# Turning raw images by products with diagonals of 1 / norm in the setup of a deformable-convolution kernel

## The chip, the core and the metric

The kernel runs on one core of one Trainium2 chip. Its time is the device time of one execution in microseconds (us). Engines are named as in the profile: PE (matmul; PEld its weight loads), DVE (vector), ACT (scalar), POOL (GpSimd) and SP (which only issues transfers here).

## The reference, cut to what matters

The input is 32 images of 64 channels and 16x16 pixels, float32. A first stage finds for every channel the partner that is least like it and normalises both together; two deformable convolution layers with batch norm follow.

```python
nrm = jnp.linalg.norm(x_flat, axis=2, keepdims=True)          # per image and channel, over 256 pixels
x_n = x_flat / jnp.maximum(nrm, 1e-12)
cos = jnp.einsum('bcn,bdn->cd', x_n, x_n) / B                  # 64x64, over all images and pixels
_, idx = jax.lax.top_k(-jnp.abs(cos).T, k)                     # k = 2, the second is the partner
gs = s + s[:, idx[:, 1:]].sum(axis=-1)                         # sums of channel and partner
gsq = sq + sq[:, idx[:, 1:]].sum(axis=-1)
...
x_hat = (x - mean) * inv                                       # then gamma, beta
# then twice: offsets by 3x3 convolution, deformable 3x3 convolution, batch norm, relu; residual at the end
```

## The kernel before, in words

Images go in pairs: the 128 partitions hold the 64 channels of one image above those of another, so there are 16 pairs ("t") of 128x256 values, read in four chunks of four pairs (`X_CHUNKS`). Everything up to the first pad of an image (L425) is called the setup here; it ends at about 26.5 us. The two layers behind it work pair by pair, their order is written out by hand, and the change doesn't touch them.

The setup has no scheduler: each engine runs its own list in the order of the code, and semaphores tie them.

- SP issues the four chunks of x, after the first one the identity matrix (64 KB), and after chunk 2 has landed the other constants.
- DVE takes statistics of each pair (`bn_stats`, L781), forms the sum of squares per chunk in three dependent steps (L788 to L793), and between the statistics of the next chunk finishes 1 / norm (L765, L768) and scales two of the four pairs (L773).
- ACT takes the root (`norm`, L404), scales the other two pairs (L410) and copies turned slabs out of PSUM (`copy_turned`, L399).
- PE, for each j of 8 (two pairs), turns the scaled slab with four 128x128 transposes (`turn`, L543) and, one j later, adds its gram products to PSUM (`gram`, L553): the order is turn(0), turn(1), gram(0), turn(2), gram(1), and so on to gram(7).
- Then a chain of small steps: the gram is copied, folded over the two images (L564), made minus its absolute value, its top 8 and their indices found (L801 to L809), the index made float (L811), compared with 0 to 63 in each half (L816), transposed on PE (L567), the identity added (L819), and the product with the sums made (L570).
- `keep_busy` makes PE multiply constants where it would otherwise wait.

One product in float32 stands in the profile as two matmul records, called passes here; a transpose stands as one.

Of the kernel before, what the change touches and what calls it, by code (L numbers as in the profile page):

```python
# [25 lines left out]
ALU = mybir.AluOpType  # L26
# [52 lines left out]
CONST_SIZES = dict(ident=P, fold=P, combine=2 * SLICE_PLACES, combine_taps=SLICE_PLACES, grid=PLACES, iota=C, edges=2)  # L79
# [26 lines left out]
def program(nc, x, consts, consts16, conv_w, conv_b, dcn_w, vecs, out):  # L106
# [3 lines left out]
    with ExitStack() as ctx:  # L110
# [38 lines left out]
        gram_sb = sb("gram_sb", [P, C])  # L149
# [3 lines left out]
        partner = sb("partner", [P, 1])  # L153
        pick = sb("pick", [P, P])
# [31 lines left out]
        iota = cst[:, CONSTS["iota"][0]:CONSTS["iota"][1]]  # L186
# [5 lines left out]
        xn = raw  # L192
        xn_t = S[:, 0, 0, :, :]

        x_in = [sem(f"x_in{i}") for i in range(X_CHUNKS)]
        ident_in = sem("ident_in")
# [9 lines left out]
        xn_by_act = sem("xn_by_act")  # L206
        xn_by_dve = sem("xn_by_dve")
# [65 lines left out]
        def _(sp):  # L273
            for g in range(X_CHUNKS):
                chunk = slice(g * CHUNK_PAIRS, (g + 1) * CHUNK_PAIRS)
                sp.dma_start(xs[:, chunk, :], x_dram[:, chunk, :]).then_inc(x_in[g], 16)
                if g == 0:
                    sp.dma_start(ident, consts[:, 0:CONSTS["fold"][0]]).then_inc(ident_in, 16)
            sp.wait_ge(x_in[X_CHUNKS - 2], 16)
            sp.dma_start(cst[:, CONSTS["fold"][0]:CONST_COLS], consts[:, CONSTS["fold"][0]:CONST_COLS]).then_inc(consts_in, 16)  # L280
# [18 lines left out]
            sp.wait_ge(cleared, 8)  # L299
# [20 lines left out]
        def _(pool):  # L320
            pool.memset(bc[:, :], 0.0).then_inc(cleared, 1)
            pool.memset(bc_centre[:, :], 0.0).then_inc(cleared, 1)
            pool.memset(pick[:, :], 0.0).then_inc(cleared, 1)
# [69 lines left out]
        def _(act):  # L393

            def copy_turned(j):
                act.wait_ge(xn_turned, j + 1)
                if j >= 2:
                    act.wait_ge(gram_step, j - 1)
                act.activation(xn_t[:, j % 2, :], build_ps[:, j % 2, :], ACT.Copy).then_inc(xn_t_ready, 1)  # L399
# [16 lines left out]
            act.wait_ge(setup_dve, 12)  # L416
# [49 lines left out]
            for layer in range(2):  # L466
                first = PAIRS * layer
                if layer == 0:
                    act.wait_ge(norm0_ready, 1)
                    act.wait_ge(cleared, 8)  # L470
# [51 lines left out]
        def _(pe):  # L522

            pe.wait_ge(ident_in, 16)

            def keep_busy(count):

                for n in range(count):
                    pe.matmul(build_ps[:, BLOCK_TAPS - 1, 0:P], ident, ident, start=True, stop=True, skip_group_check=True)  # L529
# [3 lines left out]
            def turn(j):  # L533
                if j == PAIRS // 2 - 1:
                    pe.wait_ge(xn_by_dve, 2 * (X_CHUNKS + 1))
                else:
# [559 lines left out]
```

## Time and profile before

| what | value |
|---|---|
| median of 3 runs | 436.92 us (436.37 to 439.23) |
| the profiled execution: its time, its span | 435.63 us, 433.8 us |
| busy share of the span: PE, DVE, ACT, POOL | 93%, 74%, 73%, 25% |
| setup: from the start to the first pad on ACT | 26.48 us |
| of it, first turn to the last gram product on PE | 9.77 to 20.56 us |

The span is the time from the first to the last instruction; the execution's own time has 1.8 us around it. Busy shares are means over the whole program, and the setup is only its first 6%, so they say nothing about which engine holds up the setup. For that one reads the timeline of each engine there.

### The profile page before, as it was taken

What the parts mean: (1) busy time and instruction counts of PE and PEld (TensorE: products, weight loads), DVE (VectorE), ACT (ScalarE), POOL (GpSimd) and SP (SyncE); (2) the same over time, 40 slices, a digit from 0 to 9 for tenths busy, and PEclk for the clock granted to TensorE, in tenths of its full rate; (3) what the DMA queues carried; (4) which work ended last, traced back from release to release, by engine and by line L of the source; (5) the groups of instructions that cost most, each with busy time, mean ns of one, the idle gap of its engine ahead of it and who ended that gap; (6) DMA issues with size and microseconds to landing.
All of it is one profiled execution on the core that took longest, in us unless ns stands there. A gap on an engine that the chain in (4) does not pass through costs nothing.

```text
span 433.8 us, 19098 instructions
## 1 busy us (share of the span) xinstructions
PE 402.1 (93%) x7707; PEld 341.6 (79%) x7707; DVE 319.0 (74%) x897; ACT 315.9 (73%) x387; POOL 110.3 (25%) x241
## 2 busy tenths in 40 slices
PE   4878999999999999999987899999999999999970
PEld 4755788888888888888865698888888888898860
DVE  4658977777888777776428888877777777777435
ACT  2537777878888888877726788888888888877735
POOL 6202422222222222217001422222222213210000
PEclk9999999999999999999999999999999999999995
DMA  6300433322111222222000231332222222223005
GB/s 216 89 2 17 74 55 50 49 46 46 34 33 35 46 46 46 48 39 40 2 3 3 57 62 39 46 48 46 46 46 46 46 43 44 45 45 40 2 3 193
DMA packets 59402, 20.78 MB, mean 48 GB/s; under 512 B 51680, under 2 KB 59184, under 8 KB 59360
## 3 DMA queue, kind: packets, MB, share of 16 engines
q1 hardware_dynamic: 54464, 17.73, 20.8%
q0 software_dynamic: 4896, 2.43, 2.2%
q8 instruction: 33, 0.54, 0.5%
q14 instruction: 9, 0.07, 0.1%
HBM read 3.28 MB, written 2.10 MB: 12 GB/s over the span
## 4 chain that ended last, share of the span: by engine, by line
PE 86%; DVE 5%; DMA 3%; ACT 2%; SPq 1%; issue 1%; DVEq 0%; ACTq 0%
PE acc_ps L688 57%; PE z_ps L662 14%; PE build_ps L646 7%; PE side_ps L608 3%; DMA moved<-conv_sb 1%; DMA xs<-in_x 1%; PE side_ps L597 1%; ACT raw L518 1%; SPq L268 1%; PE acc_ps L553 1%; PE build_ps L543 1%; DVE bstats L781 1%; PE side_ps L586 1%; DVE feats L901 0%; ACT S L464 0%
## 5 line engine op out<-in xcount | busy, mean ns | idle before, releaser
L688 PE MATMUL acc_ps<-S,Z 64*64 64x256 f32 x4608 | 291.2, 377 | 1.3 <-ACT S L464 0.9
L688 PEld LDWEIGHTS acc_ps<-S,Z 64*64 64x64 f32 x4608 | 220.6, 133 | 37.4 <-issue 7.0
L457 ACT ACTIVATE S<-build_ps,minus 128x1024 f32<-128x1024 f32 x190 | 201.2, 1110 | 44.2 <-PE build_ps L646 44.2
L662 PE MATMUL z_ps<-wz,xflat 64*64 64x192 f32 x1536 | 107.0, 325 | 0.0
L662 PEld LDWEIGHTS z_ps<-wz,xflat 64*64 64x64 f32 x1536 | 82.8, 132 | 4.5 <-issue 0.4
L450 ACT ACTIVATE Z<-z_ps 128x768 f32<-128x768 f32 x96 | 78.0, 813 | 5.4 <-PE z_ps L662 5.4
L915 DVE TENSOR_SCALAR S<-build_ps 128x512 f32<-128x512 f32 x96 | 65.9, 686 | 18.2 <-PE build_ps L646 16.0
L268 POOL DMA_DIRECT2D moved<-conv_sb x140 | 70.5, 511 | 21.9 <-POOL conv_sb L357 15.8
L646 PE MATMUL build_ps<-feat_rows,cst 64*64 64x512 f16 x576 | 68.7, 379 | 1.1 <-ACT feat_rows L484 1.1
L917 DVE TENSOR_SCALAR S<-build_ps 128x512 f32<-128x512 f32 x96 | 65.3, 680 | 0.0
L922 DVE COPY raw<-acc_ps 128x256 f32 (+1 forms) x32 | 13.6, 424 | 66.3 <-PE acc_ps L688 66.3
L357 POOL TENSOR_TENSOR conv_sb<-conv_sb,cst 128x32 f32<-128x32 f32 x28 | 7.4, 263 | 183.4 <-ACT conv_sb L444 183.4
L646 PEld LDWEIGHTS build_ps<-feat_rows,cst 64*64 64x64 f16 x576 | 29.5, 106 | 8.1 <-issue 2.1
L444 ACT ACTIVATE conv_sb<-side_ps,bc_centre 128x256 f32<-128x256 f32 x28 | 13.3, 474 | 23.6 <-PE side_ps L608 23.0
L369 POOL COPY xflat<-xpad 128x256 f32<-128x256 f32 x32 | 12.9, 403 | 68.7 <-PE z_ps L662 34.8
L608 PEld LDWEIGHTS side_ps<-cst,moved 64*64 64x64 f32 x448 | 22.6, 134 | 4.8 <-issue 3.1
L901 DVE TENSOR_TENSOR feats<-col_code,row_sign 128x288 f16<-128x288 f16 x64 | 26.2, 450 | 0.0
L869 DVE TENSOR_TENSOR flags<-near,cst 128x1152 f16<-128x1152 f16 x32 | 24.2, 756 | 0.0
L608 PE MATMUL side_ps<-cst,moved 64*64 64x36 f32 x448 | 22.0, 220 | 2.2 <-DMA moved<-conv_sb 2.2
L597 PE MATMUL side_ps<-xpad,wc 64*64 64x256 f32 x112 | 21.4, 377 | 0.0
L529 PE MATMUL build_ps<-cst 128*128 128x128 f32 x74 | 10.9, 308 | 4.6 <-DMA cst<-in_consts 4.6
L924 DVE TENSOR_TENSOR raw<-raw,acc_ps 128x256 f32 (+1 forms) x32 | 13.5, 421 | 1.1
(105 smaller groups left out, 274.6 us busy)
## 6 DMA issues: line engine op xcount, KB each, us to landing
xs<-in_x SPq DMA_DIRECT2D x4, 512.0 KB, 6.9
out<-raw SPq DMA_DIRECT2D x7, 256.0 KB, 2.5
moved<-conv_sb POOLq DMA_DIRECT2D x56, 11.2 KB, 1.7
moved<-conv_sb SPq DMA_DIRECT2D x56, 11.2 KB
moved<-conv_sb POOLq DMA_DIRECT2D x56, 11.3 KB, 1.6
wz<-in_dcn_w POOLq DMA_DIRECT2D x2, 288.0 KB, 4.7
feat_rows<-feats SPq DMA_TRANSPOSE x30, 3.7
moved<-conv_sb SPq DMA_DIRECT2D x28, 12.0 KB
```

The source lines that it names most:

```text
L268: eng.dma_start(moved[rows, max(0, -by):HW - max(0, by)], conv_sb[rows, max(0, by):HW + min(0, by)]).then_inc(shifted, 16)
L450: act.activation(Z[:, (parity + b) % 2, :, :, :].rearrange("p i h c -> p i (h c)"), z_ps[:, :, 0:HALVES * BLOCK_COLS], ACT.Copy).then_inc( ...
L457: act.activation(S[:, (parity + b) % 2, half, 0:ACT_TAPS, :], build_ps[:, 0:ACT_TAPS, :], ACT.Relu, bias=minus2[:, :], scale=1.0 if half = ...
L597: mm = pe.matmul(side_ps[halves[i], 0, :], wc[halves[i], layer, WC_COLS:WC_COLS + C], xpad[parity][halves[i], 1:H + 1, 1:W + 1], start=Tru ...
L608: mm = pe.matmul(place_ps[halves[i], :, n, :], moved[halves[i], n * C:(n + 1) * C], combine_taps[halves[i], :], start=True, stop=True)
L646: mm = pe.matmul(build_ps[halves[c], j, :], masks[j % 2][halves[r], halves[c]], feat_rows[halves[r], parity, b * SLICES:(b + 1) * SLICES, ...
L662: mm = pe.matmul(z_ps[halves[c], i, h * BLOCK_COLS:(h + 1) * BLOCK_COLS], xflat[parity][halves[i], pixels], wz[halves[i], layer, h, b * BL ...
L688: mm = pe.matmul(acc_ps[halves[i], g, 0:HW], Z[halves[g], slot, i, half, j * C:(j + 1) * C], S[halves[g], slot, half, j, :].rearrange(by_i ...
L869: ins = dve.tensor_tensor(flags[:, :, :, :].rearrange("p t a (n e) -> p (t a) n e", e=2), near[:, :, :, :].rearrange(by_axis).unsqueeze(2) ...
L901: ins = dve.tensor_tensor(taken[:, :, :, at:at + 8], col_code[:, :, :].rearrange(by_slot, j=BLOCK_TAPS), row_sign[:, :, a:a + 1].rearrange ...
L915: dve.tensor_scalar(S[:, slot, 0, ACT_TAPS, :], build_ps[:, ACT_TAPS, :], -2.0, 0.0, ALU.add, ALU.max).then_inc(S_by_dve, 1)
L917: dve.tensor_scalar(S[:, slot, 1, ACT_TAPS, :], build_ps[:, ACT_TAPS, :], 2.0, 0.0, ALU.add, ALU.min).then_inc(S_by_dve, 1)
```

## The change

Nothing is scaled any more. For each pair DVE makes a 64-column diagonal matrix of 1 / norm in each half of the partitions (`diags`, one operation per chunk), and `turn` multiplies raw 64x64 tiles of x by it, so that a product both turns and scales. A turn is now 16 products of 64x64 tiles in place of 4 transposes of 128x128, written to two PSUM regions in turn (`build_ps`, `z_ps`), and a gram step is 16 products of 64x64 tiles in place of 8 with 128 rows. The tile position is (half of rows i, half of columns c). The gram has two partial sums, folded by two products. DVE waits for the fold matrix before the first statistics; it finishes chunk 0's norms before it waits for chunk 1. On ACT the scaling is gone, and `norm(g + 1)` stands behind both copies of chunk g. Behind the index search, one operation writes partner plus half into 128 columns, one product with the identity turns it, and one operation compares it with the row number and adds the identity. POOL clears one tile less.

```diff
-        xn = raw
+        diags = raw[:, :, 0:C]
         xn_t = S[:, 0, 0, :, :]
+        turned_x = (build_ps[:, 0:2, 0:HW], z_ps[:, :, 0:HW])
...
             norm(0)
             for g in range(X_CHUNKS - 1):
-                act.wait_ge(rinv_step, 2 * (g + 1))
-                for t in (g * CHUNK_PAIRS + 2, g * CHUNK_PAIRS + 3):
-                    act.activation(xn[:, t, :], xs[:, t, :], ACT.Copy, scale=rinv[:, t:t + 1]).then_inc(xn_by_act, 1)
-                norm(g + 1)
                 copy_turned(2 * g)
                 copy_turned(2 * g + 1)
+                norm(g + 1)
...
             def turn(j):
+                pe.wait_ge(diags_ready, j // 2 + 1)
                 if j >= 2:
                     pe.wait_ge(xn_t_ready, j - 1)
-                for i in range(2):
-                    for h in range(HALVES):
-                        q = 2 * i + h
-                        mm = pe.transpose(build_ps[:, j % 2, q * P:(q + 1) * P],
-                                          xn[:, 2 * j + i, h * P:(h + 1) * P], ident)
+                for t in range(2):
+                    for n in range(2):
+                        for c in range(2):
+                            for i in range(2):
+                                at = (2 * n + c) * C
+                                mm = pe.matmul(turned_x[j % 2][halves[c], i, (2 * t + n) * C:(2 * t + n + 1) * C],
+                                               xs[halves[i], 2 * j + t, at:at + C], diags[halves[i], 2 * j + t, :],
+                                               start=True, stop=True)
                 mm.then_inc(xn_turned, 1)
 
             def gram(j):
                 pe.wait_ge(xn_t_ready, j + 1)
-                for q in range(4):
-                    for i in range(2):
-                        at = q * P + i * C
-                        slab = xn_t[:, j % 2, at:at + C]
-                        mm = pe.matmul(acc_ps[i * C:(i + 1) * C, 0, 0:C], slab, slab, start=(j == 0 and q == 0),
-                                       stop=(j == PAIRS // 2 - 1 and q == 3))
+                for n in range(4):
+                    for r in range(2):
+                        for i in range(2):
+                            slab = xn_t[halves[r], j % 2, i * HW + n * C:i * HW + (n + 1) * C]
+                            mm = pe.matmul(acc_ps[halves[i], r, 0:C], slab, slab, start=(j == 0 and n == 0),
+                                           stop=(j == PAIRS // 2 - 1 and n == 3))
                 mm.then_inc(gram_step, 1)
...
-            pe.matmul(side_ps[:, 0, 0:C], fold, gram_sb[:, :], start=True, stop=True).then_inc(gram_step, 1)
-            keep_busy(6)
-            pe.wait_ge(setup_dve, 8)
-            pe.transpose(side_ps[:, 1, 0:P], pick[:, :], ident).then_inc(gram_step, 1)
+            for r in range(2):
+                mm = pe.matmul(side_ps[:, 0, 0:C], fold, gram_sb[:, r, :], start=(r == 0), stop=(r == 1))
+            mm.then_inc(gram_step, 1)
+            keep_busy(5)
+            pe.wait_ge(setup_dve, 6)
+            pe.matmul(side_ps[:, 1, 0:P], partner[:, :], ident, start=True, stop=True).then_inc(gram_step, 1)
...
-                    for t in ((chunk.start + part - 2,) if g < X_CHUNKS - 1 else
-                              (chunk.start + 2 * part - 4, chunk.start + 2 * part - 3)):
-                        dve.tensor_scalar(xn[:, t, :], xs[:, t, :], rinv[:, t:t + 1], None, ALU.mult).then_inc(xn_by_dve, 1)
+                    dve.tensor_tensor(diags[:, chunk, :], fold[:, 0:C].unsqueeze(1).broadcast_to([P, CHUNK_PAIRS, C]),
+                                      rinv[:, chunk].unsqueeze(2).broadcast_to([P, CHUNK_PAIRS, C]),
+                                      ALU.mult).then_inc(diags_ready, 1)
+            dve.wait_ge(fold_in, 16)
             for g in range(X_CHUNKS):
+                if g == 1:
+                    for part in range(3):
+                        invert_norms(0, part)
                 dve.wait_ge(x_in[g], 16)
                 for n in range(CHUNK_PAIRS):
                     ins = dve.bn_stats(bstats[:, chunk.start + n, :], xs[:, chunk.start + n, :])
-                    if g >= 1:
-                        normalise(g - 1, n)
+                    elif g >= 2:
+                        invert_norms(g - 1, n)
...
-            dve.tensor_copy(partner[:, :], top8_at[:, GROUP - 1:GROUP]).then_inc(setup_dve, 1)
-            for i in range(2):
-                rows = slice(i * C, (i + 1) * C)
-                dve.tensor_scalar(pick[rows, rows], iota[rows, :], partner[rows, :], None, ALU.is_equal).then_inc(setup_dve, 1)
-            dve.tensor_tensor(pick_t[:, :], side_ps[:, 1, 0:P], ident, ALU.add).then_inc(setup_dve, 1)
+            dve.tensor_scalar(partner[:, :], top8_at[:, GROUP - 1:GROUP].broadcast_to([P, P]), half_row, None,
+                              ALU.add).then_inc(setup_dve, 1)
+            dve.scalar_tensor_tensor(out=pick_t[:, :], in0=side_ps[:, 1, 0:P], scalar=row, in1=ident,
+                                     op0=ALU.is_equal, op1=ALU.add).then_inc(setup_dve, 1)
```

The first place is ACT's list in the setup (`rinv` is 1 / norm, `S` the copied slabs, `raw` the scaled images). Before:

```order
L404 ACTIVATE rinv<-sums 128x4
L410 ACTIVATE raw<-xs,rinv 128x256 x2
L404 ACTIVATE rinv<-sums 128x4
L399 ACTIVATE S<-build_ps 128x512 x2
L410 ACTIVATE raw<-xs,rinv 128x256 x2
L404 ACTIVATE rinv<-sums 128x4
```

With the change:

```order
L404 ACTIVATE rinv<-sums 128x4
L399 ACTIVATE S<-build_ps 128x512
L399 ACTIVATE S<-z_ps 128x512
L404 ACTIVATE rinv<-sums 128x4
L399 ACTIVATE S<-build_ps 128x512
L399 ACTIVATE S<-z_ps 128x512
L404 ACTIVATE rinv<-sums 128x4
```

The root of chunk g + 1 stood ahead of the two copies of chunk g, and now stands behind them.

The second place is PE's list from the `keep_busy` at its start. Before:

```order
L529 MATMUL build_ps<-cst 128x128 x10
L543 MATMUL build_ps<-cst,raw 128x128 x8
L553 MATMUL acc_ps<-S 64x64 x8
L543 MATMUL build_ps<-cst,raw 128x128 x4
L553 MATMUL acc_ps<-S 64x64 x8
```

With the change (L540 is the turn, L551 the gram; `raw` holds the diagonals):

```order
L526 MATMUL build_ps<-cst 128x128 x10
L540 MATMUL build_ps<-raw,xs 64x64 x16
L540 MATMUL z_ps<-raw,xs 64x64 x16
L551 MATMUL acc_ps<-S 64x64 x16
L540 MATMUL build_ps<-raw,xs 64x64 x16
L551 MATMUL acc_ps<-S 64x64 x16
```

The order of turns and grams stays; a turn has 16 products for 4 transposes and a gram 16 products for 8.

The third place is DVE's list at chunk 3, between the statistics (L784) of its four pairs, with the change:

```order
L784 BN_STATS bstats<-xs 128x6
L765 TENSOR_SCALAR rinv<-rinv 128x4
L784 BN_STATS bstats<-xs 128x6
L768 RECIPROCAL rinv<-rinv 128x4
L784 BN_STATS bstats<-xs 128x6
L771 TENSOR_TENSOR raw<-cst,rinv 128x4x64
```

Where two scalings of 128x256 stood (L773 before), there is one operation for all four diagonals (L771), behind the same two statistics.

## Rows read from the trace of the kernel before

**Rows 1.** The page, parts 2 and 4: granted clock by slice; the chain that ended last.

```profile
PEclk9999999999999999999999999999999999999995
...
PE 86%; DVE 5%; DMA 3%; ACT 2%; SPq 1%; issue 1%; DVEq 0%; ACTq 0%
```

**Rows 2.** Transfers of x, by their source line: issue times; us from issue to landing.

```profile
L276 SPq DMA_DIRECT2D xs<-in_x x4: 434/478/507, 0.7 to 2.8; - x4
...
DMA to landing us min/median/max: 3.7/6.9/9.1
```

**Rows 3.** Timeline of SP: start, length (us), engine, line, what.

```profile
10.14 0.34 SPq L280 DMA_DIRECT2D cst<-in_consts  x1
```

**Rows 4.** Timeline of DVE in the setup, same columns; in brackets idle time and its releaser.

```profile
4.41 1.41 DVE L781 BATCH_NORM_STATS2 bstats<-xs 128x6 f32<-128x256 f32 x4 [4.41 <-DMA xs<-in_x]
...
7.66 0.43 DVE L781 BATCH_NORM_STATS2 bstats<-xs 128x6 f32<-128x256 f32 x1 [1.17 <-DMA xs<-in_x]
...
9.63 0.16 DVE L788 TENSOR_TENSOR squares<-bstats 128x8 f32<-128x8 f32 x1
...
10.03 0.16 DVE L793 TENSOR_TENSOR sums<-squares 128x4 f32<-128x4 f32 x1
...
15.78 0.17 DVE L765 TENSOR_SCALAR rinv<-rinv 128x4 f32<-128x4 f32 x1 [0.39 <-ACT rinv L404]
15.99 0.18 DVE L768 RECIPROCAL rinv<-rinv 128x4 f32<-128x4 f32 x1
...
22.55 0.15 DVE L811 CAST partner<-top_at 128x1 f32<-128x1 uint32 x1
22.74 0.53 DVE L816 TENSOR_SCALAR pick<-cst,partner 64x64 f32<-64x64 f32 x2
23.76 0.29 DVE L819 TENSOR_TENSOR pick_t<-side_ps,cst 128x128 f32<-128x128 f32 x1 [0.49 <-PE side_ps L567]
```

**Rows 5.** Timeline of ACT in the setup.

```profile
10.46 1.08 ACT L399 ACTIVATE S<-build_ps 128x512 f32<-128x512 f32 x2
...
15.56 0.19 ACT L404 ACTIVATE rinv<-sums 128x4 f32<-128x4 f32 x1
...
19.22 0.60 ACT L399 ACTIVATE S<-build_ps 128x512 f32<-128x512 f32 x1 [0.60 <-PE build_ps L543]
```

**Rows 6.** Timeline of PE in the setup and the first convolution behind it.

```profile
4.60 3.95 PE L529 MATMUL build_ps<-cst 128*128 128x128 f32 x20 [4.60 <-DMA cst<-in_consts]
...
12.37 0.66 PE L543 MATMUL build_ps<-cst,raw 128*128 128x128 f32 x4 [0.58 <-DVE raw L773]
12.96 0.69 PE L553 MATMUL acc_ps<-S 128*64 128x64 f32 x16
13.57 0.66 PE L543 MATMUL build_ps<-cst,raw 128*128 128x128 f32 x4
...
19.12 1.44 PE L553 MATMUL acc_ps<-S 128*64 128x64 f32 x32
20.89 0.43 PE L564 MATMUL side_ps<-gram_sb,cst 128*128 128x64 f32 x2 [0.33 <-DVE gram_sb L798]
21.16 1.56 PE L529 MATMUL build_ps<-cst 128*128 128x128 f32 x12
...
27.22 1.18 PE L586 MATMUL side_ps<-xpad,wc 128*32 128x256 f32 x24 [0.61 <-ACT xpad L425]
...
29.58 0.88 PE L662 MATMUL z_ps<-wz,xflat 64*64 64x192 f32 x16
```

**Rows 7.** Groups of PE by shape, 0 to 36 us: count, busy us, mean ns of one, idle.

```profile
L553 PE MATMUL acc_ps<-S 128*64 128x64 f32 x128 | 5.5, 228 | 0.3 <-ACT S L399 0.2
...
L662 PE MATMUL z_ps<-wz,xflat 64*64 64x192 f32 x32 | 1.8, 335 | 0.0
...
L586 PE MATMUL side_ps<-xpad,wc 128*32 128x64 f32 x16 | 0.6, 218 | 0.0
```

**Rows 8.** A group of DVE by shape, whole run, same columns.

```profile
L924 DVE TENSOR_TENSOR raw<-raw,acc_ps 128x256 f32 x20 | 8.4, 421 | 0.7
```

**Rows 9.** Waits of PE, whole run: us in total, times, longest us.

```profile
PE side_ps L751 <- DVE bmv L973: 3.1, 2, 2.1
```

More of the change, by code:

```diff
@@ L77 @@
 BN_OPS = 7
-CONST_SIZES = dict(ident=P, fold=P, combine=2 * SLICE_PLACES, combine_taps=SLICE_PLACES, grid=PLACES, iota=C, edges=2)
+CONST_SIZES = dict(fold=P, ident=P, combine=2 * SLICE_PLACES, combine_taps=SLICE_PLACES, grid=PLACES, row=1, half=1, edges=2)
 CONST_ENDS = list(accumulate(CONST_SIZES.values()))
@@ L185, in program @@
         evens = cst16[:, 3 * P:CONST16_COLS].rearrange("p (n e) -> p n e", e=2)
-        iota = cst[:, CONSTS["iota"][0]:CONSTS["iota"][1]]
+        row = cst[:, CONSTS["row"][0]:CONSTS["row"][1]]
+        half_row = cst[:, CONSTS["half"][0]:CONSTS["half"][1]]
         taken = feats[:, :, 0:BLOCK_TAPS, :]
@@ L398, in copy_turned @@
                     act.wait_ge(gram_step, j - 1)
-                act.activation(xn_t[:, j % 2, :], build_ps[:, j % 2, :], ACT.Copy).then_inc(xn_t_ready, 1)
+                act.activation(xn_t[:, j % 2, :].rearrange("p (i n) -> p i n", i=2), turned_x[j % 2], ACT.Copy).then_inc(xn_t_ready, 1)
             def norm(g):
@@ L522, in _ @@
         def _(pe):
-            pe.wait_ge(ident_in, 16)
+            pe.wait_ge(fold_in, 16)
             def keep_busy(count):
                 for n in range(count):
-                    pe.matmul(build_ps[:, BLOCK_TAPS - 1, 0:P], ident, ident, start=True, stop=True, skip_group_check=True)
+                    pe.matmul(build_ps[:, BLOCK_TAPS - 1, 0:P], fold, fold, start=True, stop=True, skip_group_check=True)
             keep_busy(10)
             def turn(j):
-                if j == PAIRS // 2 - 1:
-                    pe.wait_ge(xn_by_dve, 2 * (X_CHUNKS + 1))
-                else:
-                    pe.wait_ge(xn_by_act if j % 2 else xn_by_dve, 2 * (j // 2 + 1))
+                pe.wait_ge(diags_ready, j // 2 + 1)
                 if j >= 2:
                     pe.wait_ge(xn_t_ready, j - 1)
-                for i in range(2):
-                    for h in range(HALVES):
-                        q = 2 * i + h
-                        mm = pe.transpose(build_ps[:, j % 2, q * P:(q + 1) * P],
-                                          xn[:, 2 * j + i, h * P:(h + 1) * P], ident)
+                for t in range(2):
[6 more added lines that the diff above has]
+                                               start=True, stop=True)
                 mm.then_inc(xn_turned, 1)
@@ L930, in _ @@
             dve.wait_ge(consts16_in, 16)
-            dve.wait_ge(cleared, 8)
+            dve.wait_ge(cleared, 7)
             for layer in range(2):
@@ L1034, in shape_constants @@
     put("grid", PLACE_SCALE * grid.reshape(P, -1))
-    put("iota", np.arange(C))
+    put("row", part[:, None])
+    put("half", part[:, None] // C * C)
     edges = np.ones((P, 2), np.float32)
```

52 lines of the change are left out of this document (23 added, 29 removed).

## The prediction, made before the changed kernel was timed

> **What bounds the kernel now.** I read the chain that ended last first: PE makes up 86% of it [rows 1]. Nearly all of that lies in the two layers, which the change leaves alone, so their 409 us (435.6 less the first 26.5) are taken as they are. What can move is the setup, and there I read the timelines of the engines side by side.
>
> The data come first. The third chunk of x has landed by 10.14, when SP goes on behind its wait for it [rows 3]; the fourth is issued at 2.8 and takes 9.1, so it lands at 11.9 [rows 2]. From 12.37 PE is back to back: turn, gram, turn start at 12.37, 12.96, 13.57, so one j costs 1.20 to 1.23 us, and the last gram ends at 19.12 + 1.44 = 20.56 [rows 6]. DVE and ACT deliver the next slab in time, because ACT takes each root ahead of the copies. So before, the setup's middle is **bound by PE**, and cheaper PE work would shorten it as long as the norms keep up. Behind 20.56 it is a chain of single small steps to 26.48.
>
> **A PE section.** I call one turn or one gram a section. Before, 16 gram passes take 0.69 with 0.23 for one alone [rows 6, 7]: 0.46 between the first and the last start, in two column tiles, so eight rounds of 0.058. Now 32 passes go over four tiles: again eight rounds, if four tiles run beside each other. For that speak two rows. Sixteen passes in four 64x64 tiles with 192 columns take 0.88 with 0.335 for one [rows 6, 7]: four rounds, three intervals of 0.18. And the convolution's 24 passes take 1.18 [rows 6]: four rounds of 256 columns at 0.213 (twice the 128-column pass of 0.107 to 0.116 below) leave 1.18 - 0.85 - 0.22 = 0.11 for its eight passes of 64 columns, two rounds of 0.055. Cheap end: eight rounds of 0.055 = 0.44. Dear end: the passes follow each other as in the gram rows, 0.058 for two or 0.029 each, whatever the tile: 32 x 0.029 = 0.93. I take the cheap side, being nearest to rows with four tiles: 0.46 and one round to the next section, **0.52**.
>
> Before, the j of 1.20 holds four transposes and eight rounds. A 128-column pass is (1.56 - 0.28) / 11 = 0.116 in the keep-busy row [rows 6], at most; so 0.46 + 0.46 = 0.93 of it is work and some 0.27 lies at two changes between 128*128 and 128*64, 0.14 each. If that gap stays, a section is 0.60 to 0.62.
> The Trainium skill's page "TensorEngine Tiling (Array Packing)", Key Properties, says that changing the tiling mode drains the engine, while changing only the tile doesn't; turns and grams now have one mode, so by it the gap goes and a section is 0.52, without it 0.61 (0.9 us later at the end).
>
> **The new chain, step by step** (times as in the trace of before):
> - The start. The first keep-busy still runs 4.60 to 8.55 [rows 6], since the same 64 KB land first. DVE waits for them: 4.60 for 4.41, +0.19 [rows 4], hidden: chunk 0's sums are ready at 4.60 + 1.41 + 0.56 (the dependent steps, 9.63 to 10.19) = 6.6, root 6.8, then two steps of 0.21 [rows 4] and the diagonals. That operation has no row; the nearest is a 128x256 sum of two tiles at 0.42 [rows 8]; bounds 0.3 to 0.5. Done at 7.75, hidden by keep-busy. Turn(0) at 8.5, turn(1) at 9.0.
> - A turn's copy begins 0.46 + 0.23 + 0.04 = 0.73 behind its start. One copy is 0.60, two in a row 1.08 [rows 5]. Copy(1) ends at about 10.3, root(1) at 10.45; DVE has chunk 1's sums at 9.7 (7.66 + four statistics at 0.33 + 0.56 for the dependent steps [rows 4]) and chunk 2 since 10.14. Statistics stand between its steps: diagonals of chunk 1 at 10.16 + 3 x 0.33 + 0.15 + 0.43 = 11.75. **Turn(2) at 11.80**, 0.57 earlier than before.
> - Now root(2) stands behind copy(3) on ACT. So turn(2), gram(1), turn(3) start at 11.80, 12.32, 12.84; copy(3) 13.57 to 14.17; root(2) to 14.27. DVE stops at its wait inside chunk 3: queued behind it are that chunk's other three statistics, its sums and all later diagonals. It goes on at 14.30: clamp, statistics, reciprocal, statistics, diagonals = 0.07 + 0.33 + 0.08 + 0.33 + 0.43. **Turn(4) at 15.60.**
> - The same again without statistics between: turn(4), gram(3), turn(5) to 17.33, copy to 17.97, root to 18.07, DVE 0.21 + 0.21 + 0.45: **turn(6) at 19.02.** PE waits about 1.7 and 1.3 us at these two places, where it waited for nothing before.
> - Turn(6), gram(5), turn(7) at 20.06, its copy 20.79 to 21.39, gram(7) 21.44 to **22.13**.
> That is 22.13 against 20.56: **+1.57**.
>
> **The small steps behind it.** Copying a gram of twice the columns: +0.06. Two more fold passes of 128 weights: 2 x 0.112 = +0.22. From 22.55 to 23.27 stand cast and two comparisons [rows 4]; one operation of 128 columns in their place, at 0.25 to 0.29 like the 128-column one [rows 4]: -0.46. A product of two passes for a transpose of one: +0.11 to 0.16. The comparison with addition equals the old addition, 0.29 [rows 4]. Sum: -0.05. The single sum for the means (0.16) lies ahead of the last gram, in DVE's wait; one clear less on POOL, 32 KB less of constants and one keep-busy product less lie beside other work. The layers start 1.5 us later and change nothing else.
>
> The sum is **+1.5 us** on the profiled execution: 435.63 + 1.5 = 437.1. That execution lies 1.3 below the median of the runs, 436.92, so the median becomes **438.4**. With sections of 0.44 to 0.62 and ten of them on the chain, 437.6 to 439.4. Change below 1%, about what a measurement of this kernel can tell from none, is called the same.
>
> **Rivals.**
> 1. **PE can't start 32 passes in 0.46 us.** In the rows of before no stretch gives PE more than one 64-column product per 0.058; in the two four-tile rows the products are wider or only eight passes follow each other, which may have stood ready. If a pass costs 0.029 whatever its tile, a section is 0.93. Twelve count (turn(0) and turn(1) then delay root(1) too): 12 x 0.41 = +4.9 more, 443.3. It decides the verdict from sections of 0.76 on. Chance 15%.
> The Trainium skill speaks for it: the same page, Instruction Overhead, puts about 60 cycles on each matmul on trn2 however few its columns. At 2.4 GHz that is 25 ns; for each of 32 passes, an estimate of 0.8 a section and 441.8 in all; if it counts products, 0.4, and my forecast stands.
> 2. **The clock falls in the new gaps.** The granted clock is full throughout the busy slices [rows 1], but the first twenty passes took 3.95 us, 0.2 each, and later ones 0.116 [rows 6]: PE starts at half speed. New waits of 1.7 and 1.3 us with 60% work between are for it; that PE waited 2.1 us at the change of layers [rows 9] with no slice of lower clock is against it. Sections of 0.93 for at least half of the chain and a slow start of the first layer: 442 to 444. Chance 4%.
> 3. **The other side: the roots aren't late.** If root and diagonals were ready whenever PE is, PE alone would count from turn(2) on: turn(7) at 11.80 + 11 x 0.52 = 17.5, its copy, gram(7) to 19.6: -1.0 on the gram and 435.9 in all. It needs ACT to take root(g + 1) ahead of copy(2g + 1), against the order of its list; or sections of 0.36 or less, below the narrowest rounds seen. Chance 4%.
>
> **How the numbers follow.** The forecast has 77%. The likeliest case's own range with 0.5 for differences between executions is 437.1 to 439.9. To hold 8 in 10 the range goes down halfway to rival 3 and up to where rival 1 begins by the smaller price: 436.4 to 441.8. Slower by over 1% is above 441.3: most of rival 1 and of rival 2, 0.15. Faster by over 1% is below 432.6: no case gives it, 0.01. The same: 0.84.
>
> **What will show it.** In the profile after: 32 passes of a turn with 0.6 to 0.7 from first start to last end, and gram behind turn after 0.5; the first diagonals near 7.8 and turn(2) near 11.8; on ACT a root directly behind each second copy; DVE idle inside chunk 3's statistics for 1.3 us with ACT's root as releaser; PE idle before turn(4) and turn(6); gram ending near 22.1, the first pad near 28.0. A turn of 1.1 would mean rival 1; passes of twice the length rival 2; no idle time before turn(4), rival 3. I'd be wrong altogether if the layers behind 28 us took another time than before.

## The result and the profile after

| | before | changed |
|---|---|---|
| median | 437.08 us (436.37 to 439.23, 4 runs) | 442.15 us (440.68 to 444.76, 4 runs) |
| ratio | | 1.0129, interval 1.0099 to 1.0159 |
| profiled execution, its span | 435.63, 433.8 us | 442.19, 439.9 us |
| first pad (end of the setup) | 26.48 | 30.72 |
| from there to the end of the span | 407.3 | 409.2 |

The changed kernel is slower by 5 us; +1.5 was forecast, and 442.15 lies 0.35 above the range. The profiled executions are 6.6 us apart, because the one of before lies 1.45 below its median. Of the 6.1 us between their spans 4.2 lie in the setup and 1.9 in the layers, where nothing was to change. The other 0.5 us lies outside the span: the time is 1.8 to 2.0 us above the span in every execution of the kernel before and 2.2 to 2.3 in every one of the changed kernel. The kernels partner_early have 2.2 to 2.4 as well, so it comes with a part of the change that they share; no run shows with which.

PE's timeline in the setup (start, length, then line, operation, tiles, count, in brackets idle time and releaser) answers to [rows 6]:

```profile
5.07 4.63 PE L526 MATMUL build_ps<-cst 128*128 128x128 f32 x20 [5.07 <-DMA cst<-in_consts]
9.64 0.99 PE L540 MATMUL build_ps<-raw,xs 64*64 64x64 f32 x32
10.46 0.64 PE L540 MATMUL z_ps<-raw,xs 64*64 64x64 f32 x32
11.36 0.69 PE L551 MATMUL acc_ps<-S 64*64 64x64 f32 x32 [0.26 <-ACT S L399]
13.19 0.69 PE L540 MATMUL build_ps<-raw,xs 64*64 64x64 f32 x32 [1.13 <-DVE raw L771]
13.70 0.65 PE L551 MATMUL acc_ps<-S 64*64 64x64 f32 x32
14.17 0.65 PE L540 MATMUL z_ps<-raw,xs 64*64 64x64 f32 x32
14.63 0.41 PE L551 MATMUL acc_ps<-S 64*64 64x64 f32 x10
16.62 0.57 PE L551 MATMUL acc_ps<-S 64*64 64x64 f32 x22 [1.58 <-issue]
17.08 0.69 PE L540 MATMUL build_ps<-raw,xs 64*64 64x64 f32 x32
...
18.52 0.35 PE L551 MATMUL acc_ps<-S 64*64 64x64 f32 x9
20.34 0.52 PE L551 MATMUL acc_ps<-S 64*64 64x64 f32 x20 [1.47 <-issue]
...
22.14 0.30 PE L551 MATMUL acc_ps<-S 64*64 64x64 f32 x7
23.75 1.04 PE L551 MATMUL acc_ps<-S 64*64 64x64 f32 x56 [1.32 <-issue]
25.20 0.66 PE L563 MATMUL side_ps<-gram_sb,cst 128*128 128x64 f32 x4 [0.40 <-DVE gram_sb L800]
```

Two things are to be seen. Sections (a turn or a gram) start 0.51, 0.47 and 0.46 apart (13.19, 13.70, 14.17, 14.63): four tiles do run beside each other. And three times PE stops in the middle of a gram, between two products of one loop that share one wait at its head, with "issue" as releaser: nothing the profile knows of. Add the passes: 20 + 6 x 32 + 10 = 222 at the first stop; 127 later the second, at 349; 127 later the third, at 476. A pass is a weight load and a matmul, two instructions; with the two semaphore waits that the trace has on the way, the distance is 256 instructions. The page has a queue that it calls "instruction", whose transfers are 0.59 MB / 36 = 16 KB each:

```profile
q8 instruction: 36, 0.59, 0.6%
```

Before it was 33 transfers: 353 more passes are 706 instructions, 2.8 pieces. None falls between 91 and 186 us or between 290 and 388, where PE repeats the body of a loop. The first begins at 13.85, and the window from 13.8 to 15.1 us has (packets, MB, share of 16 engines):

```profile
q8 instruction: 1, 0.02, 5.8%
```

PE returns at 16.62, 2.8 us after this transfer began and 1.6 after it ended. The next two begin at 17.77 and 21.54, and PE returns 2.6 and 2.2 us later. It is so at all 29 stops at the end of a piece in the traces of this case: PE goes on 2.2 to 2.8 us after a transfer of 16 KB begins and 1.2 to 1.6 after it ends. So **PE runs out of program**. It happens again in the first pair of the layers, where before there was no such row (the transfer begins at 49.88, 2.4 us ahead of PE's return):

```profile
52.29 1.96 PE L689 MATMUL acc_ps<-S,Z 64*64 64x256 f32 x32 [2.67 <-issue]
```

DVE and ACT show the late roots as forecast (DVE's rows first, then ACT's, whose last is the first pad):

```profile
11.92 0.17 DVE L765 TENSOR_SCALAR rinv<-rinv 128x4 f32<-128x4 f32 x1 [1.49 <-ACT rinv L404]
...
15.60 0.34 DVE L765 TENSOR_SCALAR rinv<-rinv 128x4 f32<-128x4 f32 x1 [1.19 <-ACT rinv L404]
...
19.50 0.17 DVE L765 TENSOR_SCALAR rinv<-rinv 128x4 f32<-128x4 f32 x1 [1.53 <-ACT rinv L404]
```

```profile
14.88 0.60 ACT L399 ACTIVATE S<-z_ps 128x512 f32<-128x512 f32 x1 [0.34 <-PE z_ps L540]
15.37 0.20 ACT L404 ACTIVATE rinv<-sums 128x4 f32<-128x4 f32 x1
...
30.72 1.09 ACT L422 ACTIVATE xpad<-xs,shift,scale 128x256 f32<-128x256 f32 x2 [0.99 <-DVE shift L834]
```

### The profile page after: what moved, and what is told of

It is laid out like the page before. It is cut to its first block, busy times and chain, and to the rows that moved or that the text cites. A ratio compares the mean times of both kernels' runs of the same rounds, so it can differ in the third digit from the quotient of the medians.

```text
span 439.9 us, 19785 instructions
## 1 busy us (share of the span) xinstructions
PE 402.6 (92%) x8060; PEld 342.7 (78%) x8060; DVE 317.4 (72%) x886; ACT 313.6 (71%) x381; POOL 110.4 (25%) x240
## 4 chain that ended last, share of the span: by engine, by line
PE 86%; DVE 5%; ACT 3%; issue 3%; DMA 1%; POOL 1%; DVEq 0%; SPq 0%; ACTq 0%
PE acc_ps L689 57%; PE z_ps L663 14%; PE build_ps L647 7%; PE side_ps L609 3%; PE side_ps L598 1%; ACT raw L515 1%; PE build_ps L526 1%; PE acc_ps L551 1%; DMA cst<-in_consts 1%; PE build_ps L540 1%; PE side_ps L587 1%; POOL moved L269 1%; DVE feats L898 1%; ACT S L454 0%; PE z_ps L540 0%
## 5 line engine op out<-in xcount | busy, mean ns | idle before, releaser
L526 PEld LDWEIGHTS build_ps<-cst 128*128 128x128 f32 x72 | 10.5, 230 | 5.5 <-DMA cst<-in_consts 5.1
```

Of the source, the lines that this page charges most:

```text
L526: pe.matmul(build_ps[:, BLOCK_TAPS - 1, 0:P], fold, fold, start=True, stop=True, skip_group_check=True)
```

## The experiments

Two theories: **program supply** (PE waits for its next 256 instructions, because it uses up a piece faster than the next one comes) and **late roots** (ACT's order). Ratios are to the kernel before, run beside each; medians of different sets of runs can differ by over 1 us for one kernel (435.83 to 437.16 for the kernel before). "Stops at 222" and the like are counts of PE passes from the start, as added above.

**roots_first**: the changed kernel with the roots ahead of the copies.

```diff
             for g in range(X_CHUNKS - 1):
+                norm(g + 1)
                 copy_turned(2 * g)
                 copy_turned(2 * g + 1)
-                norm(g + 1)
```

> The changed kernel with ACT's root of chunk g + 1 ahead of the two copies of chunk g. Two theories of the 4.2 us that the gram ends later (24.80 for 20.56). Late roots alone: with the roots in time PE never waits between turn(2) and gram(7); turn(2) at about 12, 13 sections of 0.49 and the last copy, gram end near 20, the time 4 to 5 us less than the changed kernel's 442.1, about 437.5. Program supply: PE stands still after 222, 349 and 476 passes because the next 256 of its instructions aren't there, each time some 2.8 us after it has passed the middle of the piece before; these stops were hidden by the late roots and are now bare: they stay at the same pass counts, gram end near 23.9, the time only about 1 us less, 441.

Measured: 443.49 us, 1.0165 (1.0122 to 1.0208), not faster at all. PE again stops after 222 passes, longer:

```profile
13.27 0.44 PE L551 MATMUL acc_ps<-S 64*64 64x64 f32 x10
17.25 0.81 PE L551 MATMUL acc_ps<-S 64*64 64x64 f32 x20 [3.54 <-issue]
```

and behind the stop the clock is granted at half for a while. By windows (length; busy us and passes in flight of PE, PEld, DVE, ACT, POOL; granted clock; DMA share; GB/s):

```profile
12.00:16.00 4.00, 1.68 (x96) 1.40 (x87) 3.49 (x17) 1.49 (x4) 0.00 (x0) 1.00 0.60 156
16.00:20.00 4.00, 2.75 (x105) 2.75 (x108) 0.13 (x2) 0.60 (x1) 2.34 (x4) 0.57 0.02 4
```

The gram ends at 25.24. Late roots alone are refuted as the cause: without them the stops take their place. The other stops came too, 0.24 us at pass 349, where PE was slower, and 1.32 at 476. My sum for the supply theory was too kind: the first transfer began only at 14.68, 1.2 us after PE's last pass had started, and I had not counted the clock. This also answers the 2.8 us "after it has passed the middle" of my expectation. In the changed kernel the three transfers began 134, 138 and 167 instructions into the piece in hand, in its second profile (after_again) 42, 53 and 116, and at the stop in the layers 256, that is behind the end of the piece, in both. Behind each of the three stops in the setup the next transfer began 1.1 to 1.2 us after PE's return, in both profiles. What starts a transfer elsewhere is not shown; the 2.2 to 2.8 us from its beginning to PE's return is.

**small_in_setup**: 16 small products in idle time behind gram(0), 52 more at the end for four keep-busy products, so that the layers keep their place.

```diff
                 turn(j)
                 gram(j - 1)
+                if j == 1:
+                    small(16)
...
-            keep_busy(9)
+            keep_busy(5)
+            small(52)
```

`small` multiplies constants, 32 columns of weights, into PSUM that nothing reads.

> The changed kernel with 16 small constant products (32 columns of weights, 32 passes) put into PE's idle time behind gram(0), and 52 more with four keep-busy products less at the end of the setup, so that the layers' instructions lie at the same places in pieces of 256 as in the changed kernel. The products themselves fit the idle time. Program supply: the stops come 32 passes earlier in the program, inside turn(3), turn(5) and turn(7) in place of gram(2), gram(4) and gram(6), and there delay the copies and roots behind them: gram end about 3 us later (near 28) and about 445 us. Any other cause of the stops (waits for copies, operands, PSUM): they stay inside gram(2) and gram(4) and the time stays within 0.5 us of 442.1.

```profile
11.11 0.46 PE L534 MATMUL build_ps<-cst 128*32 128x32 f32 x32
12.32 0.69 PE L547 MATMUL build_ps<-raw,xs 64*64 64x64 f32 x32 [0.74 <-DVE raw L781]
12.83 0.65 PE L558 MATMUL acc_ps<-S 64*64 64x64 f32 x32
13.30 0.39 PE L547 MATMUL z_ps<-raw,xs 64*64 64x64 f32 x10
15.03 0.71 PE L547 MATMUL z_ps<-raw,xs 64*64 64x64 f32 x20 [1.34 <-issue]
```

The stop moved from gram(2) into turn(3), again at pass 222 of the program as it now is: it belongs to the instruction's number, not to what the instruction does. Of the three stops foreseen in the setup only this one came: the clock behind it was half until 22 us, with sections 0.85 to 0.91 apart, and the roots came later still, which I take to have given the next pieces time. The gram ended at 25.80 and not at 28. The time, 443.59 us, 1.0149 (1.0106 to 1.0193), is not clear of the changed kernel's (1.0099 to 1.0159); the place of the stop is the evidence here, not the time.

**before_layer_shift** and **after_layer_shift**: the same filler at the end of the setup moves the layers within the pieces, in the kernel before to where the changed kernel has them, and the other way round.

```diff
# before_layer_shift
-            keep_busy(9)
+            keep_busy(5)
+            small(52)
# after_layer_shift
-            keep_busy(9)
+            keep_busy(6)
+            small(19)
```

> The kernel before, with four keep-busy products at the end of the setup replaced by 52 small ones, so that its layers lie in the 256-instruction pieces of the program as the changed kernel's do (within 2). Nothing else is touched. Program supply: the 2.67 us stop that the changed kernel has between L609 and L689 at 49.6 us appears in this one at the same place (near 45.5), and the time is about 2 us more than before, 439. If the layers' 1.9 us in the changed kernel came from later or different data or from chance, nothing moves: 437.

> The changed kernel with three keep-busy products at the end of the setup replaced by 19 small ones: the layers lie in the 256-instruction pieces as in the kernel before (within 2). Program supply: the stop of 2.67 us at 49.6 is gone or below 1, the setup keeps its stops, and the time is about 2 us less than the changed kernel's, 440. Otherwise 442.

In the shifted kernel before, the stop appears, in the same first pair, with the clock behind it at 0.64 from 48 to 52 us:

```profile
46.65 2.49 PE L696 MATMUL acc_ps<-S,Z 64*64 64x256 f32 x28 [1.83 <-issue]
```

```profile
44.00:48.00 4.00, 2.02 (x32) 1.20 (x30) 2.80 (x9) 1.76 (x3) 2.92 (x6) 0.94 0.19 44
48.00:52.00 4.00, 4.00 (x56) 3.13 (x50) 1.55 (x4) 1.73 (x3) 0.00 (x0) 0.64 0.02 6
```

Its median didn't move as expected: 437.14 us, 1.0011 (0.9987 to 1.0034); seven of its ten runs lie at 435.7 to 437.2, three at 439.3 to 439.4, the profiled one (439.36) among these; the mean clock of these three is 0.983 to 0.985, of the seven 0.986 to 0.990. So the place of the stop is as the theory says, and its price was wrong: the filled kernel lost next to nothing but in those three. Part of the price is that the stop takes the place of a wait for `moved` transfers a little later, which the kernel before has and the two kernels with the stop have not:

```profile
50.43 0.66 PE L608 MATMUL side_ps<-cst,moved 64*64 64x36 f32 x16 [0.77 <-DMA moved<-conv_sb]
```

The changed kernel without the stop: 441.03 us, 1.0093 (1.0060 to 1.0126), no idle row at that place, and 407.6 us from first pad (31.02) to end (438.6), as before the change (407.3). So in the profiles the shift gives back 1.6 of the layers' 1.9 us, and the stop less the wait it replaced (2.67 - 0.77) is as much as the whole 1.9. Other waits in the layers went both ways: 0.2 to 0.4 more at three places in the first pairs, 0.9 less for `moved` in the second layer. Between medians it is 1.1 us, with overlapping intervals, so the time alone doesn't show it; that the layers take 1.7 us more in the second profiles too (409.2 for 407.4) does.

**gram_tall**: gram products of 128 rows as before, on the new layout.

```diff
                 for n in range(4):
-                    for r in range(2):
-                        for i in range(2):
-                            slab = xn_t[halves[r], j % 2, i * HW + n * C:i * HW + (n + 1) * C]
+                    for i in range(2):
+                        slab = xn_t[:, j % 2, i * HW + n * C:i * HW + (n + 1) * C]
```

> The changed kernel with the gram as before the change: 8 products with 128 rows of weights in place of 16 of 64x64, one partial sum and one fold product; the new layout of the slabs and the late roots stay. PE's program is 65 products shorter, 260 instructions, one piece of 256 almost exactly, so the layers keep their place in the pieces. Program supply: the stops at passes 222 and 349 now fall in turn(4) and turn(7), both reached late because of the roots, so they vanish or stay under 0.3 us; each j costs 0.27 more for two changes of tile mode. Gram end about 24.5 (24.80 changed), small steps -0.3, time 441.5. If 64x64 gram products as such made the stops, they'd be gone as well and nothing tells it apart here; the next run does.

Measured: 440.86 us, 1.0098 (1.0067 to 1.0129). No stop in the setup; PE waits only for diagonals, 1.34, 1.44 and 1.07 us. As expected. The gram ends at 24.54 for 24.80: with the late roots still there, it gains next to nothing that the stops are gone. (The stop in the first pair stayed, 1.31 us.)

**roots_gram_tall**: both edits.

> The changed kernel with both edits: roots ahead of the copies, and the gram in 8 products of 128 rows. Program supply: 48 passes a j are still more than the supply gives in the setup, so two stops remain, at pass 222 inside turn(4) and at 349 inside turn(7), of 1 to 3 us each, though no 64x64 gram product is left; gram end 22.5 to 24, time 439.5 to 441. If only roots and the form of the gram cost time: no stop, gram end near 20.2, time 437.3.

Measured: 440.81 us, 1.0112 (1.0068 to 1.0156). One stop, at 222 inside turn(4), though no 64x64 gram product is left; then half the clock (the gram's 16 passes take 1.12 for 0.69):

```profile
16.80 0.36 PE L540 MATMUL build_ps<-raw,xs 64*64 64x64 f32 x6 [1.78 <-issue]
17.08 1.12 PE L550 MATMUL acc_ps<-S 128*64 128x64 f32 x16
```

The second of the two expected stops didn't come; I put that down to the slow clock, which gave the next piece time, but no run shows it alone. The gram ended at 23.63.

**short_busy**: 5 keep-busy products first, DVE's wait for the fold matrix later (and 5 small products at the end of the setup to keep the layers' place).

```diff
-            keep_busy(10)
+            keep_busy(5)
```

> The changed kernel with 5 keep-busy products at its start in place of 10 (5 small ones at the end of the setup keep the layers' place in the pieces), and DVE's wait for the fold matrix moved behind the first chunk's statistics. In the changed kernel turn(0) stood behind the keep-busy until 9.64 though its diagonals were there at 8.16. Late start: turn(0) near 8.3, root(1) about 1 us earlier, and by the chain through the roots turn(2), turn(4), turn(6) each about 1 us earlier: 441. If the stops for instructions set the pace (their lead counts from PE's own progress, which also moves forward), the same gain; if they count from when the loads of x and of the weights end, no gain: 442.

Turn(0) started at 8.16 (1.5 earlier), turn(2) at 12.15 and the first pad came at 29.68, both 1.0 earlier than in the changed kernel's first profile. That shows nothing of the edit: in the second profile of the unchanged one (after_again, below) turn(2) also starts at 12.15 and the first pad comes at 29.45. The time didn't move: 442.47 us, 1.0142 (1.0108 to 1.0176); the profiled execution had its stop of 2.38 in the first pair and half the clock behind it.

**after_again, before_again, roots_late_wz**: second profiles of both kernels, and roots_first with the loads of weights held back.

```diff
-            pool.wait_ge(x_in[X_CHUNKS - 2], 16)
+            pool.wait_ge(gram_step, 3)
```

> The changed kernel unchanged, for a second profile of it. Program supply: the stops are at the same passes again (222, 349, 476 and 846), with no or small differences in length; its time 441 to 444, and where the granted clock falls to half behind one of the stops, near the upper end. If the stops were chance, they lie elsewhere.

> The kernel before unchanged, for a second profile of it. In all profiles but the first the first 64 KB of constants landed at 5.0 to 5.2 us and PE's first 20 passes took 4.6 us in place of 3.95. If that is chance of the execution and not of the change, it is so here too, and the first pad stays within 0.5 us of 26.5, because the kernel before has slack there (turn(0) waited until 9.77).

> The kernel with the roots ahead of the copies (443.5), and POOL's loads of the deformable weights held back until the third gram is done in place of the third chunk of x. In that kernel the stop at pass 222 was 3.54 us, while 1.3 to 1.6 elsewhere; the loads of weights lay over it. If the reload of the program queues behind those loads, the stop at 222 shrinks to 1.5 to 2, the clock stays up, and the time is 1.5 to 3 us less, 441. If the length has another reason, it stays above 3.

After_again: 442.66 us, 1.0187 (1.0169 to 1.0205), above the first interval, so the change costs 1.3 to 1.9% by the set of runs. Stops at 222, 349, 476 and 846 again, of 0.77, 0.85, 1.56 and 2.66 us, at the same instructions:

```profile
8.91 0.69 PE L540 MATMUL build_ps<-raw,xs 64*64 64x64 f32 x32
...
12.15 0.69 PE L540 MATMUL build_ps<-raw,xs 64*64 64x64 f32 x32 [1.13 <-DVE raw L771]
...
14.78 0.57 PE L551 MATMUL acc_ps<-S 64*64 64x64 f32 x22 [0.77 <-issue]
...
22.48 1.04 PE L551 MATMUL acc_ps<-S 64*64 64x64 f32 x56 [1.56 <-issue]
```

Before_again: one run, 435.09 us, keep-busy 4.64 us from 4.63, first pad at 25.66. The keep-busy took 3.92 in after_again and 4.03 in small_in_setup (my expectation left that one out), so its length and start are chance of the execution. Roots_late_wz: 442.81 us, 1.0173 (1.0114 to 1.0233). The transfer ahead of pass 222 began at 12.28 for 14.68 and the stop shrank from 3.54 to 0.95, as a queue shared with the loads would make it. But the next two were 1.83 and 1.86, the clock was half from 24.5 to 27.9, and nothing was gained.

**roots_wide_tall**: less program for more PE work. Roots first, tall gram, the layers shifted as in after_layer_shift, and turns with 128 columns of weights:

```diff
-                        for c in range(2):
-                            for i in range(2):
-                                at = (2 * n + c) * C
-                                mm = pe.matmul(turned_x[j % 2][halves[c], i, (2 * t + n) * C:(2 * t + n + 1) * C],
-                                               xs[halves[i], 2 * j + t, at:at + C], diags[halves[i], 2 * j + t, :],
+                        for i in range(2):
+                            mm = pe.matmul(turned_x[j % 2][:, i, (2 * t + n) * C:(2 * t + n + 1) * C],
+                                           xs[halves[i], 2 * j + t, n * P:(n + 1) * P], diags[halves[i], 2 * j + t, :],
```

> The changed kernel with a program for PE that is slower by itself and shorter: roots ahead of the copies, turns by 8 products with 128 columns of weights (64 rows) in place of 16 of 64x64, gram by 8 products of 128 rows, and the layers shifted in the pieces of 256 instructions as in after_layer_shift. A turn takes 0.9 for 0.48, so PE's own work for one j rises from 0.98 to 1.6 us, while its instructions halve, 128 to 64 a j. Program supply: 128 instructions then take 3.2 us, longer than the 2.8 of a reload, so no stop but perhaps a part of the first, gram end near 22.6 (24.8 in the changed kernel), first pad near 28.2, time 438. If PE's work sets the pace: 8 turns with 0.42 more each, so later than roots_gram_tall (23.9), about 27, and the time 442 or more.

```profile
12.64 1.11 PE L545 MATMUL build_ps<-raw,xs 64*128 64x64 f32 x16
13.68 0.69 PE L555 MATMUL acc_ps<-S 128*64 128x64 f32 x16
14.29 1.11 PE L545 MATMUL z_ps<-raw,xs 64*128 64x64 f32 x16
15.33 0.69 PE L555 MATMUL acc_ps<-S 128*64 128x64 f32 x16
15.95 1.11 PE L545 MATMUL build_ps<-raw,xs 64*128 64x64 f32 x16
```

438.36 us, 1.0057 (1.0039 to 1.0075). One j now costs PE 1.65 us for 0.98, not one stop, the gram ends at 23.40 for 24.80, and the whole is 4.3 us below the changed kernel in the same set of runs (442.66). Two thirds more time per j on the bounding engine, half the instructions, and faster: an account by PE's work alone can't give that. A piece now lasts four j, 6.6 us, for two j and 2.0 us in the changed kernel; that, and not the half piece of my expectation, is to be set against the time that a piece takes to come. Three edits are in this step together, though. Roots_gram_tall, the nearest kernel, has one stop and a gram that ends at 23.63, so the wide turns did little for the gram itself; and with no stop and no late root the kernel is still 0.6% slower than before.

**late_wide_tall**: the same with the late roots, where no stop in the setup can cover them.

> roots_wide_tall with the one difference that ACT's roots stand behind the copies again, as in the changed kernel. PE's program is the short one, so no stop for instructions can cover what the late roots cost. Late roots as a cause of their own: turn(2) starts at about 14.2 for 12.6, and from turn(2) to turn(4) and from turn(4) to turn(6) it takes 5.0 and 4.5 us for 3.3, so the gram ends 4 to 4.5 us later, 442.5 for 438.4. If the late roots cost nothing and the stops are the whole cause: 438.4 again.

```profile
13.23 1.11 PE L545 MATMUL build_ps<-raw,xs 64*128 64x64 f32 x16 [1.42 <-DVE raw L775]
...
16.08 1.12 PE L555 MATMUL acc_ps<-S 128*64 128x64 f32 x16
18.36 1.97 PE L545 MATMUL build_ps<-raw,xs 64*128 64x64 f32 x16 [1.16 <-DVE raw L775]
```

```profile
12.00:19.00 7.00, 4.61 (x70) 4.18 (x72) 4.36 (x18) 1.29 (x3) 2.34 (x4) 0.76 0.30 72
19.00:26.00 7.00, 6.38 (x72) 5.84 (x72) 1.09 (x6) 1.29 (x3) 0.00 (x0) 0.50 0.00 0
26.00:33.00 7.00, 6.67 (x78) 6.13 (x77) 0.32 (x2) 1.19 (x2) 0.00 (x0) 0.50 0.01 2
```

449.43 us, 1.0309 (1.0262 to 1.0356). Turn(2) to turn(4) takes 5.13 for 3.31 (5.0 was expected, without the half clock that is in it from 15.7 on). The clock fell behind the first idle stretch and stayed at half past the end of the gram, which comes 8.4 us later (31.78 for 23.40), twice the expected loss; the whole is 11 us longer. So the late roots are a cause of their own, by the waits and by what the clock does behind them. The slowest of the four executions, 453.68 us, has a mean clock of 0.989, the others 0.964 to 0.968: what made that one long isn't the clock, and it has no profile.

Put together: roots in time alone, 1.0165; no stop in the setup alone, 1.0098; both, with one stop left, 1.0112; both without a stop in the setup, 1.0057. In the changed kernel the two causes lie over each other, so that taking away one hardly helps.

**partner_early, partner_early_again**: the kernel before with two parts of the change, the partner by one product and one comparison, and chunk 0 finished before the wait for chunk 1.

```diff
+                if g == 1:
+                    for part in range(4):
+                        normalise(0, part)
...
-                    if g >= 1:
+                    if g >= 2:
                         normalise(g - 1, n)
```

(and the hunks on `partner`, `pick`, `row` and `half` of the change, without the second partial gram)

> The kernel before with two parts of the change alone: the partner by one product and one comparison, and chunk 0's norms and scaling on DVE ahead of the wait for chunk 1. PE's program grows by 4 instructions less 4. Partner part: from the end of the index search to the product on PE 0.34 for 0.78, one pass more 0.1: -0.3. Early chunk 0: DVE is 0.6 us earlier from chunk 1 on, turn(2) at 11.8 and the gram end at about 20.0 for 20.56: -0.6. Together -0.9, 436.2. If the layers' own differences between executions (up to 2 us) hide it: 436 to 438, no verdict.

> partner_early once more (the kernel before with the partner part and the early first chunk), because its interval, 0.9966 to 1.0004, just touched one. If the 0.15% are real: below one again, about 0.6 us.

435.50 us, 0.9985 (0.9966 to 1.0004), and again 435.87 us, 0.9978 (0.9963 to 0.9994): 0.2% faster than the kernel before, at the edge of what the runs can tell. In the profile of partner_early PE idles 0.39 ahead of the partner's product for 0.61, and the first pad comes at 26.21 for 26.48; the gram ends at 20.50 for 20.56, so of the early chunk hardly anything arrived in that execution, whose turn(0) started at 9.64 behind its keep-busy. The unchanged kernel's first pads lie 0.8 apart (26.48 and 25.66), so the 26.21 proves nothing.

## Why the prediction was wrong, step by step

The profiled execution came out 6.6 us longer and not 1.5. Setup: 4.2 for 1.5. Layers: 1.9 for nothing. Outside the span: 0.5 for nothing.

- **A section, 0.52: right.** 0.51, 0.47, 0.46. The gap between tile modes is gone when turn and gram share one; in gram_tall, where they don't, the starts lie 0.62 apart.
- **The chain through the roots: right.** Turn(2) to turn(4) 3.89 (3.80 forecast), turn(4) to turn(6) 3.56 (3.42); in after_again 3.70 and 3.31. In both profiles stops lie inside these stretches, so part of the agreement is luck; gram_tall has the waits without a stop, 1.44 and 1.07 us (1.7 and 1.3 forecast). The diagonals' operation took 0.42 as its nearest row; the small steps behind the gram came to 5.92 us in both kernels (-0.05 forecast). That the late roots cost of themselves late_wide_tall shows.
- **The start, turn(0) at 8.5: wrong by 1.1 in this execution.** Keep-busy began at 5.07 and ran 4.63, its passes 0.21 apart, where later ones in the setup of before are at most 0.116 apart. I saw one execution's 8.55 and took it as fixed. Before_again had the long one too (4.64), its turn(0) started at 9.07 and turn(2) at 11.58, which waited for its operands as before. In after_again turn(0) starts at 8.91, and the forecast times come out within 0.4 us: turn(2) 12.15 (11.80 forecast), turn(4) 15.85 (15.60), turn(6) 19.16 (19.02). So the start explains the first profile, and not the change: after_again's first pad still comes 3.8 us behind before_again's.
- **Gram(7) right behind its copy, 22.13: the failed step.** "Turn(7) at 20.06, its copy, gram(7)" put the supply of PE's instructions at nothing without a reason. Before, a j had 20 passes in 1.2 us, so 256 instructions lasted some 7.7 us (an estimate from the rows of before); now a j has 64 passes in 0.98, so they would be gone in 2.0, and from one return of PE to the next it took 3.7 and 3.4 us. The stops in gram(2) and gram(4) lay under the waits for roots (the diagonals for turn(4) were ready at 17.02, turn(4) began at 17.08). The third held gram(6) until 23.75, when the last copy had been ready since 22.98; gram(7) began 1.1 us later than it could, and the gram ended 1.1 later. In after_again it is 1.3 of the 1.4 us that the gram ended behind the forecast (23.52 for 22.13).
- **"The layers start 1.5 us later and change nothing else": failed too,** and with it the prediction's own sign of being wrong, that the layers take another time. PE's program grew by 353 passes, which moved the layers within the pieces and put a stop of 2.67 us into the first pair. By after_layer_shift it is worth 1.6 us between profiles; the 1.1 between medians isn't clear of noise.
- **The range** ended at 441.8, a price worked out from the page named below; no run shows that price.
- **Rival 1 had the time (441.8 to 443.3) but not the mechanism:** it priced each pass, and the passes cost nothing extra. The Trainium skill's "TensorEngine Tiling (Array Packing)", Instruction Overhead, taken for each pass in whatever tile, is not what the trace shows: 32 passes start within 0.46 us, 0.015 each.
- **Rival 2, the clock, is real** though not in the changed kernel's profiled execution: it fell in or behind a stop in roots_first, roots_gram_tall, roots_late_wz, small_in_setup, short_busy, gram_tall and before_layer_shift, and in late_wide_tall, without a stop, for some 20 us. I had given it 4%.
- **Rival 3** needed the roots in time; with them in time (roots_first) the stops took the gain.

## What to carry to other kernels

Count the instructions an engine gets through per microsecond, not only its busy time: a straight-line stretch of small float32 products can need its program faster than it comes, and the profile shows it as idle "issue" at equal distances in the instruction count. Cheaper work on the bounding engine can be worth nothing when it is cut into more products; here, with the roots in time and the layers shifted back, half as many products that took two thirds more time together won 4 us back. A step that lengthens a program moves all that lies behind it within the reloaded pieces, so a part that wasn't touched can change, and two causes that lie over each other hide one another until both are taken away. Profile both kernels twice before explaining 1 us: the unchanged ones differed by 0.8 and 1.3 us at the first pad.

## What the runs showed of the hardware

- PE's stops lie 256 instructions or a multiple of it apart, and with each goes a transfer of 16 KB. Their places depend on the count alone (222, 349, 476 and 846 passes in both profiles of the changed kernel; 222 in six other kernels). Whether there is one depends on how fast PE uses up the piece, and on when the transfer begins: PE goes on 2.2 to 2.8 us after that, at all 29 stops. When it begins is not explained; with the loads of weights under way it was at 14.68 and the stop 3.54 us, with the loads held back at 12.28 and 0.95. In the layers it began as late as the end of the piece.
- 32 float32 passes over four 64x64 tiles start within 0.46 us, and between a 64x64 and a 128x64 section PE loses about 0.15 us (starts 0.62 apart in gram_tall, 0.47 without the change of mode).
- A stop or idle stretch of 1.3 to 3.5 us is now and then followed by a granted clock of half, 0.57 to 0.64 in a 4 us window; a stop of 2.67 us was not, in both profiles of the changed kernel. Which executions it hits differs. In before_layer_shift it goes with the three slow ones by their mean clocks. It does not explain the spread of roots_gram_tall, 438.4 to 443.0 us: the execution with the half clock is the 439.48 one, with the lowest mean clock of the four (0.984), and those of 442.14 and 443.01 have 0.987 and 0.985. What made them long stays open.
